# VectorE's order in the opening and the second group's period of a graph block, with two masks and two residual products moved from GpSimd

## The chip, the cores and the metric

The kernel runs on one core of one Trainium2 chip. The metric is the device time of one execution in microseconds (us). The kernel before takes 381.16 us, the median of three runs (380.99 to 382.29).

## The reference

32 graphs of 256 nodes with 128 features go through two blocks, each closed by a residual sum and a LayerNorm. `_layernorm` is without weights. Cut to what matters:

```
xc = transpose(x)                                              # block 1
h = relu(bn1(conv1(xc)));  h = bn2(conv2(h))                   # 1x1, then 17 taps over the nodes
x_conv = transpose(relu(h + xc))
s = x @ w_se.T + b_se                                          # 3 columns
A = exp(-(|s_n|^2 + |s_m|^2 - 2 s_n.s_m)) * adj
x_nmp = A @ relu(x @ w_msg.T + b_msg)
gi = [x_conv, x_nmp] @ w_ih.T + b_ih;  gh = x @ w_hh.T + b_hh
r, z = sigmoid(gi_r + gh_r), sigmoid(gi_z + gh_z);  n = tanh(gi_n + r * gh_n)
x = layernorm(x + (1 - z) * n + z * x)
h = relu(((1 + eps) * x + adj @ x) @ W1 + b1)                  # block 2
x = layernorm(x + h @ W2 + b2)
```

## The kernel before

The graphs go in 8 groups of 4, so 1024 columns, in two halves of 512 (`h` is 0 or 1). A period of the kernel (`steady(s)`) works on three groups at once: gates, normalisation and block 2 of group `s - 1` (`gb`), convolution and message part of group `s` (`gm`), and the first convolution of group `s + 1` (`gf`). `run` (L445) gives each engine `prologue()`, `steady(1)`, `steady(2)`, a hardware loop with two periods in it that runs twice, `steady(7)` and `last`. The order on each engine is written out by hand, and the engines meet at semaphores alone: `wait(engine, NAME, group, count)` and `done(instruction, NAME)`.

The 17 taps are computed from seven smaller sums (HALF, ZERO, PLUS2, MINUS2, PLUS1, MINUS1, INF), each with its stream of input differences (`sv`) and its 4 or 5 weights. Most products are made of three: an input is split into a high part (`sth`, `wh`, ScalarE's `stream_high`, `tap_high`) and the rest (`stl`, `wl`, VectorE's `stream_low`, `tap_low`), which costs one subtraction on VectorE with both inputs in SBUF. In the opening (group 0, and three sums of groups 1 and 2) TensorE uses the whole numbers (`plain_taps`, L1380); the low parts of the taps' weights are made in the first and second period, and TensorE waits for them by `w_low`, whose counts follow `W_ORDER` (L208).

The names that the change and the prediction touch:

- Masks: `exps` (ScalarE, L697) writes the exponentials. For groups 1 to 7 they stay in PSUM (`front`) and VectorE's `mask` (L968) multiplies them with `adjT` into `amat`. For group 0 they go to `amat` in SBUF and GpSimd's `first_mask` (L568) multiplies there. TensorE's `nmp` (L1441, `front<-amat,msg`) needs them.
- Residual product: `residual` (GpSimd, L552), `xw<-xw,xv`; VectorE's `gates_end` (L1043, L1046) needs it, and TensorE's `y_transpose` (L1495) needs that.
- Other work of GpSimd: `streams1`, `streams2` (L532, L533), `rsqrt` (L547, a power), `x_low1` (L573), `add_b2` (L562), `token_diffs` (L523, L525), `add_diagonal` (L581).
- VectorE: `reset` (L1032), `add_input` (L1038), `y_stats` (L1053, L1057), `y_apply` (L1075), `inf_stream` (L924, L928), `pair2_sum` (L991), `u_sum` (L981), `pair2_add` (L999, L1000), `pair1_sum` (L1004), `pair1_add` (L1012), `inf_add` (L1017), `xconv_low` (L1022), `nmp_low` and `stream_low` (L862), weights' low parts (L1115), sums for the opening's weights (L1159).
- TensorE: three-part products (L1327) of the gates (`back`, 27 of 512 columns for each half) and of the sums (`conv`, 12 or 15 of 256 columns), `aggregate` (L1441, `back<-adjT,xn`).

Order of TensorE in a period: HALF, ZERO, PLUS2, messages, gates of half 0, factors, gates of half 1, transpose of half 0, MINUS2, PLUS1, transpose of half 1, MINUS1, two distances, aggregate of both halves, two distances, INF, the MLP (with `conv1` of the next group between), `nmp` of both halves. The first three of these belong to the opening for group 1.

## Time and profile before

| | us |
| --- | --- |
| median of three runs | 381.16 |
| the profiled execution | 381.71 |
| its span, first to last instruction | 379.8 |
| TensorE busy | 363.1 (96%) |
| VectorE busy | 319.2 (84%) |
| ScalarE busy | 231.5 (61%) |
| GpSimd busy | 162.1 (43%) |
| share of TensorE in the chain that ended last | 66% |
| share of VectorE in it | 23% |

The granted clock of TensorE is 0.998 of full speed. The times of single instructions are from the profiled execution, from the start of its span. The end of a matmul is modelled, so matmuls overlap in the rows, and the distance from start to start tells what one costs. The opening lasts until the gates of group 0 start, at 43.7 us; the second group's period lasts from there to some 84.7 us, with its three opening sums of the next group to 91.6 us. The periods after it take 44 us each.

### The profile page before, as it was taken

To read this page: it belongs to the slowest core of one execution; us is meant where nothing else is said; L and a number is where in the kernel's file an instruction comes from. 1 tells how busy PE (TensorE), PEld (TensorE's weight loads), DVE (VectorE), ACT (ScalarE), POOL (GpSimd) and SP (SyncE) were. 2 spreads that over 40 slices of the span, in tenths; PEclk is the share of its full clock that TensorE was granted. 3 is DMA by queue.
4 is the path that set the end of the run, shared out by engine and by line. 5 is a ranking of instruction groups with operands and counts; after the bars stand their busy time and mean duration, and the time that the engine had idled before them with its cause. 6 is when DMAs were issued, how large, how long until landed. Compare 5 with 4: busy or idle time off the path is not lost.

```text
span 379.8 us, 6436 instructions
## 1 busy us (share of the span) xinstructions
PE 363.1 (96%) x2150; PEld 316.3 (83%) x2150; DVE 319.2 (84%) x702; ACT 231.5 (61%) x436; POOL 162.1 (43%) x162
## 2 busy tenths in 40 slices
PE   6999998899999999999999999999999999999994
PEld 4777887688898988899898998989888998988973
DVE  4999999998799987979699786998789886995584
ACT  3464773645767467664866567774676648564765
POOL 3125334446342653527323463517525373234362
PEclk9999999999999999999999999999999999999999
DMA  5700004300113010130112000120101201000002
GB/s 195 269 3 0 0 3 166 112 1 24 33 55 112 0 58 1 55 112 3 55 57 90 22 28 28 55 110 0 55 0 55 110 3 55 2 0 2 0 30 83
DMA packets 8135, 19.39 MB, mean 51 GB/s; under 512 B 688, under 2 KB 5168, under 8 KB 7088
## 3 DMA queue, kind: packets, MB, share of 16 engines
q1 hardware_dynamic: 7536, 18.17, 13.8%
q10 hardware_dynamic: 576, 0.92, 0.7%
q8 instruction: 13, 0.21, 0.2%
q14 instruction: 10, 0.08, 0.1%
HBM read 14.90 MB, written 4.19 MB: 50 GB/s over the span
## 4 chain that ended last, share of the span: by engine, by line
PE 66%; DVE 23%; issue 5%; DMA 3%; ACT 2%; POOL 1%; SPq 0%; ACTq 0%; DVEq 0%
PE back L1327 26%; PE conv L1327 17%; PE back L1441 6%; PE conv L1380 3%; DVE stats L1053 3%; PE back L1539 3%; DMA xv<-in_x_dram 3%; DVE stl L862 3%; PE front L1413 2%; DVE tail L1088 2%; PE back L1495 2%; PE front L1433 1%; DVE nmpl L862 1%; DVE sv L890 1%; DVE xn L1075 1%
## 5 line engine op out<-in xcount | busy, mean ns | idle before, releaser
L1327 PE MATMUL conv<-sth,wh 128*128 128x256 f32 x207 | 62.5, 302 | 1.3 <-DVE stl L862 1.2
L1327 PE MATMUL conv<-sth,wl 128*128 128x256 f32 x207 | 59.0, 285 | 0.0
L1327 PE MATMUL conv<-stl,wh 128*128 128x256 f32 x207 | 58.9, 284 | 0.0
L547 POOL TENSOR_TENSOR rstd<-rstd,small 128x4 f32<-128x4 f32 (+1 forms) x34 | 38.3, 1126 | 41.6 <-DVE rstd L1057 41.0
L1327 PEld LDWEIGHTS conv<-sth,wh 128*128 128x128 f32 x207 | 39.1, 189 | 3.5 <-DVE stl L862 1.2
L552 POOL TENSOR_TENSOR xw<-xw,xv 128x512 f32<-128x512 f32 (+1 forms) x17 | 21.2, 1246 | 47.9 <-ACT xw L720 47.9
L1327 PEld LDWEIGHTS conv<-stl,wh 128*128 128x128 f32 x207 | 39.1, 189 | 0.2
L1327 PEld LDWEIGHTS conv<-sth,wl 128*128 128x128 f32 x207 | 39.1, 189 | 0.0
L652 ACT ACTIVATE sth<-sv 128x272 fp32r<-128x272 f32 (+1 forms) x33 | 17.3, 523 | 35.6 <-DVE sv L890 20.9
L737 ACT ACTIVATE tail<-tail,shift,rstd 128x128 f32<-128x128 f32 x60 | 24.1, 482 | 11.2 <-DVE shift L1110 11.2
L581 POOL TENSOR_TENSOR adjT<-adjT,diag 128x256 f32<-128x256 f32 x32 | 27.9, 901 | 6.5 <-DVE msg L936 4.3
L1441 PE MATMUL back<-adjT,xn 128*128 128x256 f32 x120 | 28.2, 387 | 2.3 <-DVE xn L1075 2.1
L523 POOL TENSOR_TENSOR av<-h 128x544 f32<-128x544 f32 x6 | 8.1, 1342 | 51.4 <-ACT h L667 51.4
L1441 PE MATMUL front<-amat,msg 128*128 128x256 f32 x128 | 29.1, 379 | 0.0
L1441 PEld LDWEIGHTS back<-adjT,xn 128*128 128x128 f32 x120 | 22.0, 190 | 6.7 <-DVE xn L1075 2.9
L1539 PEld LDWEIGHTS back<-later_w,tail 128*128 128x128 f32 x224 | 26.3, 192 | 0.7
L1539 PE MATMUL back<-later_w,tail 128*128 128x128 f32 x224 | 26.5, 275 | 0.0
L744 ACT ACTIVATE tail<-back,first_w 128x512 f32<-128x512 f32 (+1 forms) x30 | 20.4, 683 | 9.7 <-PE back L1327 9.7
L1441 PEld LDWEIGHTS front<-amat,msg 128*128 128x128 f32 x128 | 23.8, 190 | 2.9
L1075 DVE TENSOR_SCALAR xn<-back,stats,rstd 128x128 f32<-128x128 f32 x60 | 20.5, 403 | 3.1 <-POOL rstd L547 2.4
L716 ACT ACTIVATE gbuf<-back,small 128x512 f32<-128x512 f32 x15 | 10.3, 690 | 19.3 <-PE back L1327 19.3
L562 POOL TENSOR_TENSOR tail<-xn,later_w 128x512 f32<-128x512 f32 x15 | 20.0, 1339 | 2.3 <-DVE xn L1075 2.3
(242 smaller groups left out, 1031.4 us busy)
## 6 DMA issues: line engine op xcount, KB each, us to landing
adjT<-in_adj_dram SPq DMA_DIRECT2D x8, 1024.0 KB, 4.9
out_dram<-tail SPq DMA_DIRECT2D x15, 256.0 KB, 2.2
xv<-in_x_dram SPq DMA_DIRECT2D x7, 512.0 KB, 3.3
tail<-in_conv_dram ACTq DMA_DIRECT2D x3, 256.0 KB, 4.6
gbuf<-in_gates_dram SPq DMA_DIRECT2D x1, 576.0 KB, 8.0
xv<-in_x_dram SPq DMA_DIRECT2D x2, 256.0 KB, 5.6
tail<-in_conv_dram SPq DMA_DIRECT2D x1, 320.0 KB, 5.4
later_w<-in_later_dram SPq DMA_DIRECT2D x1, 320.0 KB, 5.1
```

Source lines behind the costliest of these rows:

```text
L547: done(pool.tensor_tensor(rstd[:, k, v, q], rstd[:, k, v, q], minus_half[:, q], ALU.pow), RSTD[k])
L552: done(pool.tensor_tensor(xw[:, h, part(c)], xw[:, h, part(c)], xv[u][:, part_cols(h, c)], ALU.mult), XWX_READY)
L562: done(pool.tensor_tensor(out_tile(h, c)[:, q, :], xn[:, h, q, :], b2bc.unsqueeze(1).to_broadcast([P, len(part_blocks(c)), D]), ALU.add), ...
L581: done(pool.tensor_tensor(dg, dg, diag[:, :].unsqueeze(1).to_broadcast([P, PAR, P]), ALU.add), ADJE_READY)
L652: done(act.activation(dst, src, ACT.Copy), name)
L737: last = act.activation(o[:, q, :], o[:, q, :], ACT.Identity, bias=shift[:, v, q:q + 1], scale=rstd[:, 1, v, q:q + 1])
L744: done(act.activation(hid[:, h, f, part(c)], bank("hid", h, c, f), ACT.Relu, bias=vec[:, B1 + f:B1 + f + 1]), HID_READY)
L862: done(dve.tensor_tensor(dst, src, full(hi), ALU.subtract), name)
L1075: last = dve.tensor_scalar(xn[:, h, q, :], src(q, q + 1), stats[:, 0, v, q, 1:2], rstd[:, 0, v, q:q + 1], ALU.subtract, ALU.mult)
L1327: ins = pe.matmul(bank, a, b, start=first and k == 0, stop=last and k == len(todo) - 1)
L1441: ins = pe.matmul(tile[:, k * N:(k + 1) * N], lhs(b, rm), rhs(b, rm), start=rm == 0, stop=rm == PAR - 1)
L1539: ins = pe.matmul(tile[:, k * P:(k + 1) * P], hid[:, h, f, q * P:(q + 1) * P], w2[:, f, :], start=f == 0, stop=f == 1)
```

## The change

On VectorE:

- The masks of graphs 2 and 3 of group 0 go from GpSimd to VectorE, which reads the exponentials from PSUM. A semaphore of its own, `first_masked`, counts GpSimd's two masks, and `nmp` of group 0 waits for both kinds.
- Both residual products of group 0 go from GpSimd to VectorE.
- In the opening `pair1_sum` comes before `pair2_add`, and the low part of PLUS1's weights goes behind `factors` of the second period. ScalarE's wait for it goes from ahead of the gates to just ahead of the write of `tz` that needs it.
- The second group's period has its own function, `second_group`, with another order. The low part of ZERO's weights goes from ahead of half 1's `reset` to behind `pair2_sum`, and `inf_stream` from behind `gates_end` of half 1 to behind the first two masks. GpSimd waits for ZERO's low part ahead of `add_b2`, and ScalarE's high part of the INF stream goes behind the first two exponentials.
- At each period's end but the seventh, `inf_add` goes from between the two `nmp_low` to directly behind `pair1_add`, `xconv_low` of parity 0 from ahead of `half_stream` to behind both `nmp_low`, and the low parts of the pair-2 streams (`stream_low(gf, 2)`) ahead of `nmp_low`.

On VectorE in the opening, from `u_sum` of group 0 (L981 before, L995 after) to the differences of group 1; before:

```order
L981 SCALAR_TENSOR_TENSOR usum<-conv,first_w,xv 128x4x64 x4
L985 SCALAR_TENSOR_TENSOR usum<-conv,first_w,usum 128x4x64
L991 SCALAR_TENSOR_TENSOR pm<-conv,first_w,pm 128x4x64 x2
L884 TENSOR_TENSOR sv<-vv 128x272
L1159 SCALAR_TENSOR_TENSOR adjT<-adjT 128x640
L877 TENSOR_TENSOR av<-h 128x4x2x68
```

And after:

```order
L995 SCALAR_TENSOR_TENSOR usum<-conv,first_w,xv 128x4x64 x4
L999 SCALAR_TENSOR_TENSOR usum<-conv,first_w,usum 128x4x64
L982 TENSOR_TENSOR amat<-front,adjT 128x512
L1005 SCALAR_TENSOR_TENSOR pm<-conv,first_w,pm 128x4x64 x2
L898 TENSOR_TENSOR sv<-vv 128x272
L1177 SCALAR_TENSOR_TENSOR adjT<-adjT 128x640
L982 TENSOR_TENSOR amat<-front,adjT 128x512
L891 TENSOR_TENSOR av<-h 128x4x2x68
```

The two masks (`amat<-front,adjT`) stand where there was none; the last weight sum of the opening (`adjT<-adjT`) stands between them.

On VectorE in the second group's period, from the last sum of the gates of half 1 (L1046 before, L1064 after) to the low part of the INF stream (`stl<-sv,sth` of 272 columns); before:

```order
L1046 TENSOR_TENSOR gbuf<-gbuf,xw 128x512
L924 SCALAR_TENSOR_TENSOR sv<-av 128x4x67
L928 SCALAR_TENSOR_TENSOR sv<-sv 128x272
L1075 TENSOR_SCALAR xn<-back,stats,rstd 128x128 x4
L1053 BN_STATS stats<-back 128x6 x2
L1057 TENSOR_SCALAR rstd<-stats 128x4
L991 SCALAR_TENSOR_TENSOR pm<-conv,first_w,pm 128x4x64 x2
L1075 TENSOR_SCALAR xn<-back,stats,rstd 128x128 x4
L862 TENSOR_TENSOR stl<-sv,sth 128x272
L968 TENSOR_TENSOR amat<-front,adjT 128x512 x2
L1115 TENSOR_TENSOR wl<-tail,wh 128x512
```

And after:

```order
L1064 TENSOR_TENSOR gbuf<-gbuf,xw 128x512
L1093 TENSOR_SCALAR xn<-back,stats,rstd 128x128 x4
L1071 BN_STATS stats<-back 128x6 x2
L1075 TENSOR_SCALAR rstd<-stats 128x4
L1005 SCALAR_TENSOR_TENSOR pm<-conv,first_w,pm 128x4x64 x2
L1133 TENSOR_TENSOR wl<-tail,wh 128x512
L1093 TENSOR_SCALAR xn<-back,stats,rstd 128x128 x4
L982 TENSOR_TENSOR amat<-front,adjT 128x512 x2
L938 SCALAR_TENSOR_TENSOR sv<-av 128x4x67
L942 SCALAR_TENSOR_TENSOR sv<-sv 128x272
L1133 TENSOR_TENSOR wl<-tail,wh 128x512
L876 TENSOR_TENSOR stl<-sv,sth 128x272
```

The two instructions of the INF stream (`sv<-av`, `sv<-sv`) went behind the normalisation and the two masks; the first `wl<-tail,wh` is ZERO's.

On VectorE at the end of a period, from the second `out_stats` to the shifts; before:

```order
L1057 TENSOR_SCALAR rstd<-stats 128x4
L862 TENSOR_TENSOR nmpl<-front,nmph 128x512
L1017 SCALAR_TENSOR_TENSOR usum<-conv,first_w,usum 128x4x64
L862 TENSOR_TENSOR stl<-sv,sth 128x544
L862 TENSOR_TENSOR nmpl<-front,nmph 128x512
L1022 SCALAR_TENSOR_TENSOR xcl<-usum,xch 128x4x128
L1110 SCALAR_TENSOR_TENSOR shift<-stats,rstd 128x4 x2
```

And after:

```order
L1075 TENSOR_SCALAR rstd<-stats 128x4
L876 TENSOR_TENSOR stl<-sv,sth 128x544
L876 TENSOR_TENSOR nmpl<-front,nmph 128x512 x2
L1036 SCALAR_TENSOR_TENSOR xcl<-usum,xch 128x4x128 x2
L1128 SCALAR_TENSOR_TENSOR shift<-stats,rstd 128x4 x2
```

The low part of the pair-2 streams comes first, `inf_add` (`usum<-conv,first_w,usum`) stands no longer here, and both `xcl` stand together.

The diff, cut to its core:

```
-        W_ORDER = ("conv1", "gates", PLUS1, MINUS2, ZERO, MINUS1, INF, "w1", HALF, PLUS2)
+        W_ORDER = ("conv1", "gates", PLUS1, MINUS2, MINUS1, ZERO, INF, "w1", HALF, PLUS2)
-        A_READY = stage("a_ready", 4)
+        A_READY = stage("a_ready", 4, 0, 2)
+        def early(g, b):
+            return opening(g) and b < 2
...
# sync, prologue
-                wait(sp, A_READY, 0, 1)
+                sp.wait_ge(first_masked, 2)
+                wait(sp, A_READY, 0, 4)
...
# gpsimd
-                for b in range(GB):
-                    first_mask(b)
+                first_mask(0)
+                first_mask(1)
...
-                residual(gb, 1 - u, 0)
-                residual(gb, 1 - u, 1)
+                if not first:
+                    residual(gb, 1 - u, 0)
+                    residual(gb, 1 - u, 1)
                 rsqrt(0, gb, 0)
                 if first:
                     x_low1(0)
                 rsqrt(0, gb, 1)
                 if first:
                     x_low1(1)
+                    pool.wait_ge(w_low, w_count(ZERO))
                 add_b2(gb, 0)
...
# scalar
-                out = amat[...] if opening(g) else fb[b % 2][:, :]
+                out = amat[...] if early(g, b) else fb[b % 2][:, :]
...
                 wait(act, Z_FULL, g, item(h, c) + 1)
+                if opening(g) and h == 0:
+                    act.wait_ge(w_low, w_count(PLUS1))
...
                 minus2_out(gm)
-                stream_high(gm, 4)
+                if not first:
+                    stream_high(gm, 4)
                 if front:
                     x_high(gf, 1 - u)
                 minus1_out(gm)
                 exps(gm, 0)
                 exps(gm, 1)
+                if first:
+                    stream_high(gm, 4)
...
# vector
+            def residual(g, u, h):
+                wait(dve, XW_READY, g, h + 1)
+                done(dve.tensor_tensor(xw[:, h, :], xw[:, h, :], xv[u][:, cols(h)], ALU.mult), XWX_READY)
...
                 u_sum(0, 0)
+                mask(0, 0, 2)
                 pair2_sum(0)
                 first_stream1(MINUS1, ALU.subtract)
                 taps_step(minus1, minus1, -1.0, even)
+                mask(0, 0, 3)
...
+                pair1_sum(0)
                 pair2_add(0)
-                pair1_sum(0)
...
+                xconv_low(0, 1)
                 x_low(0, 0, 1)
-                tap_low(PLUS1)
-                xconv_low(0, 1)
+            def second_group():
+                messages(1, 0); messages(1, 1); messages(1, 2); factors(1)
+                tap_low(PLUS1); reset(0, 0); parts1(1)
+                add_input(0, 0); residual(0, 0, 0); gates_end(0, 0)
+                stream_low(1, 2); tap_low(MINUS2); stream_low(1, 3); tap_low(MINUS1)
+                reset(0, 1); add_input(0, 1); y_stats(0, 0); residual(0, 0, 1); gates_end(0, 1)
+                y_apply(0, 0); y_stats(0, 1); pair2_sum(1); tap_low(ZERO); y_apply(0, 1)
+                mask(1, 1, 0); mask(1, 1, 1); inf_stream(1); tap_low(INF); stream_low(1, 4)
+                h_low(0, 0); w_low_part(w1l...); h_low(0, 1)
+                mask(1, 1, 2); mask(1, 1, 3); u_sum(1, 1); pair1_sum(1)
...
                 pair1_add(gm, 1)
+                inf_add(gm)
...
                     out_stats(gb, 0)
-                    xconv_low(gm, 0)
                     half_stream(gf)
                     zero_stream(gf)
                     stream_low(gf, 0)
                     parts2(gf)
                     stream_low(gf, 1)
                     out_stats(gb, 1)
+                    stream_low(gf, 2)
                     nmp_low(gm, 0)
-                    inf_add(gm)
-                    stream_low(gf, 2)
                     nmp_low(gm, 1)
+                    xconv_low(gm, 0)
                     xconv_low(gm, 1)
...
# tensor
                 if opening(g):
-                    wait(pe, E_READY, g, h + 3)
-                    wait(pe, A_READY, g, 2 * h + 2)
-                else:
-                    wait(pe, A_READY, g, h + 3)
+                    pe.wait_ge(first_masked, 2)
+                wait(pe, A_READY, g, h + 3)
```

In the diff several calls of `second_group` stand on one line here; in the kernel each has its own.

## Rows read from the trace of the kernel before

**Rows 1.** windows of the steady periods, one period (stretch, its us, busy us of each engine, clock).

```profile
135.90:180.00 44.10, 43.91 (x274) 38.97 (x273) 36.99 (x83) 28.37 (x54) 19.73 (x19) 1.00 0.14 49
```

**Rows 2.** chain that ended last (start us, us, what).

```profile
151.08 3.65 PE conv L1327 x30
...
181.75 6.24 PE back L1327 x27
```

**Rows 3.** TensorE's waits (engine line <- waited for: us, times, longest).

```profile
PE back L1441 <- DVE xn L1075: 2.1, 2, 1.4
...
PE conv L1327 <- DVE stl L862: 1.2, 5, 0.4
```

**Rows 4.** timeline of TensorE (start us, us, what, idle before it and its releaser).

```profile
31.93 2.41 PE L1380 MATMUL conv<-sv,adjT 128*128 128x256 f32 x10 [0.95 <-DVE adjT L1159]
...
62.11 0.63 PE L1495 MATMUL back<-ident_w,gbuf 128*128 128x128 f32 x4 [1.16 <-DVE gbuf L1046]
...
71.61 0.39 PE L1327 MATMUL conv<-sth,wh 128*128 128x256 f32 x1
...
89.31 2.41 PE L1380 MATMUL conv<-sv,first_w 128*128 128x256 f32 x10 [0.74 <-issue]
```

**Rows 5.** timeline of VectorE in the opening.

```profile
28.71 1.27 DVE L884 TENSOR_TENSOR sv<-vv 128x272 f32<-128x272 f32 x1
29.90 1.88 DVE L1159 SCALAR_TENSOR_TENSOR adjT<-adjT 128x640 f32<-128x640 f32 x1
...
35.64 1.25 DVE L1000 SCALAR_TENSOR_TENSOR usum<-pm,usum 128x512 f32<-128x512 f32 x1
```

**Rows 6.** timeline of GpSimd in the opening.

```profile
25.93 5.18 POOL L568 TENSOR_TENSOR amat<-amat,adjT 128x512 f32<-128x512 f32 x4 [9.87 <-ACT amat L697]
```

**Rows 7.** timeline of VectorE in the second group's period.

```profile
50.17 1.26 DVE L1032 SCALAR_TENSOR_TENSOR gbuf<-gbuf 128x512 f32<-128x512 f32 x1
...
52.15 1.87 DVE L1115 TENSOR_TENSOR wl<-adjT,wh 128x640 fp32r<-128x640 f32 x1
...
57.17 1.92 DVE L1115 TENSOR_TENSOR wl<-adjT,wh 128x640 fp32r<-128x640 f32 x1
...
61.27 0.69 DVE L1046 TENSOR_TENSOR gbuf<-gbuf,xw 128x512 f32<-128x512 f32 x1
...
62.35 1.41 DVE L928 SCALAR_TENSOR_TENSOR sv<-sv 128x272 f32<-128x272 f32 x1
63.68 1.36 DVE L1075 TENSOR_SCALAR xn<-back,stats,rstd 128x128 f32<-128x128 f32 x4
64.95 0.75 DVE L1053 BATCH_NORM_STATS2 stats<-back 128x6 f32<-128x256 f32 x2
...
68.31 1.44 DVE L862 TENSOR_TENSOR stl<-sv,sth 128x272 fp32r<-128x272 f32 x1
69.67 1.28 DVE L968 TENSOR_TENSOR amat<-front,adjT 128x512 f32<-128x512 f32 x2
```

**Rows 8.** timeline of GpSimd there.

```profile
57.06 1.34 POOL L552 TENSOR_TENSOR xw<-xw,xv 128x512 f32<-128x512 f32 x1 [3.73 <-ACT xw L720]
...
62.03 1.43 POOL L573 TENSOR_TENSOR xl<-xv,xh 128x512 fp32r<-128x512 f32 x1
...
68.18 2.70 POOL L562 TENSOR_TENSOR tail<-xn,later_w 128x512 f32<-128x512 f32 x2
```

**Rows 9.** timeline of VectorE at a period's end.

```profile
176.69 0.48 DVE L1017 SCALAR_TENSOR_TENSOR usum<-conv,first_w,usum 128x256 f32<-128x256 f32 x1
177.08 0.72 DVE L862 TENSOR_TENSOR stl<-sv,sth 128x544 fp32r<-128x544 f32 x1
```

**Rows 10.** timeline of ScalarE there and in the gates after it.

```profile
175.98 0.66 ACT L652 ACTIVATE sth<-sv 128x544 fp32r<-128x544 f32 x1 [1.97 <-POOL sv L533]
...
184.57 0.69 ACT L713 ACTIVATE gbuf<-back,small 128x512 f32<-128x512 f32 x1
```

**Rows 11.** timeline of TensorE there.

```profile
177.85 0.39 PE L1327 MATMUL conv<-sth,wh 128*128 128x256 f32 x1 [0.19 <-DVE stl L862]
```

More of the change, by code:

```diff
@@ L804, in steady @@
                     msg_out(gm, k)
[L805 to L806 removed]
+                first = isinstance(s, int) and s == 1
                 gates(gb, 0)
@@ L1205, in prologue @@
                 w_low_part(wl[:, S_GATE:S_GATE + 9, :], graw, wh[:, S_GATE:S_GATE + 9, :], w_count("gates"))
+                xconv_low(0, 1)
                 x_low(0, 0, 1)
-                tap_low(PLUS1)
-                xconv_low(0, 1)
+            def second_group():
+                messages(1, 0)
+                messages(1, 1)
+                messages(1, 2)
+                factors(1)
+                tap_low(PLUS1)
+                reset(0, 0)
+                parts1(1)
+                add_input(0, 0)
+                residual(0, 0, 0)
+                gates_end(0, 0)
+                stream_low(1, 2)
+                tap_low(MINUS2)
+                stream_low(1, 3)
+                tap_low(MINUS1)
+                reset(0, 1)
+                add_input(0, 1)
+                y_stats(0, 0)
+                residual(0, 0, 1)
+                gates_end(0, 1)
+                y_apply(0, 0)
+                y_stats(0, 1)
+                pair2_sum(1)
+                tap_low(ZERO)
+                y_apply(0, 1)
+                mask(1, 1, 0)
+                mask(1, 1, 1)
+                inf_stream(1)
+                tap_low(INF)
+                stream_low(1, 4)
+                h_low(0, 0)
+                w_low_part(w1l[:, :], w1raw, w1h[:, :], w_count("w1"))
+                h_low(0, 1)
+                mask(1, 1, 2)
+                mask(1, 1, 3)
+                u_sum(1, 1)
+                pair1_sum(1)
@@ L1210, in steady @@
             def steady(s, u, front):
                 gb, gm, gf = s - 1, s, s + 1
-                first, second = isinstance(s, int) and s == 1, isinstance(s, int) and s == 2
-                for k in range(3):
-                    messages(gm, k)
-                factors(gm)
-                parts1(gm)
-                if first:
-                    stream_low(gm, 2)
-                reset(gb, 0)
-                add_input(gb, 0)
-                if first:
-                    tap_low(MINUS2)
@@ L1223, in steady @@
-                gates_end(gb, 0)
-                stream_low(gm, 3)
-                if first:
-                    tap_low(ZERO)
-                    reset(gb, 1)
-                    tap_low(MINUS1)
-                else:
+                if isinstance(s, int) and s == 1:
+                    second_group()
+                else:
+                    for k in range(3):
+                        messages(gm, k)
+                    factors(gm)
+                    parts1(gm)
+                    reset(gb, 0)
+                    add_input(gb, 0)
+                    gates_end(gb, 0)
+                    stream_low(gm, 3)
@@ L1232, in steady @@
                     reset(gb, 1)
[L1233 to L1257 removed]
+                    add_input(gb, 1)
+                    y_stats(gb, 0)
+                    gates_end(gb, 1)
+                    y_apply(gb, 0)
+                    y_stats(gb, 1)
+                    pair2_sum(gm)
+                    y_apply(gb, 1)
+                    stream_low(gm, 4)
+                    mask(gm, u, 0)
+                    mask(gm, u, 1)
+                    h_low(gb, 0)
+                    pair1_sum(gm)
+                    h_low(gb, 1)
+                    mask(gm, u, 2)
+                    mask(gm, u, 3)
                 if front:
@@ L1263, in steady @@
                 pair1_add(gm, 1)
-                if second:
+                inf_add(gm)
+                if isinstance(s, int) and s == 2:
                     tap_low(HALF)
```

43 lines of the change are left out of this document (10 added, 33 removed).

## The prediction

> **What bounds the kernel now.** I first read the windows. In a steady period of 44.1 us TensorE is busy for 43.9, at full granted clock, and VectorE for 37.0 [rows 1]. So from the third group on only what TensorE still waits for can be won. The chain of waits shows what TensorE costs there: 30 matmuls of 256 columns take 3.65 us, 0.122 each, and 27 of 512 columns take 6.24, 0.231 each [rows 2]. The list of TensorE's waits then names the two that matter beyond the opening: five times the low part of a stream, 1.2 us in all, and twice the normalised `xn`, 2.1 us [rows 3]. The timeline gives their places. TensorE stands before MINUS1 of the opening (0.95), before the second transpose of the second group's period (1.16), and before PLUS2 of group 2 (0.74) [rows 4]; the two waits for `xn` lie between the transpose at 62.11 and INF at 71.61. The bound is thus TensorE, with VectorE's order in front of it up to some 90 us.
>
> Why VectorE is late there stands in rows 5 to 8. `sv<-vv` on 272 columns takes 1.27 us and the weight sum after it 1.88 [rows 5], while GpSimd multiplies its four masks for 5.18 us [rows 6]; alone, such operations take 0.44 and 0.83 (the same forms elsewhere in the trace). The pattern repeats in the second group: 1.26, 1.87, 1.92, 1.41 and 1.44 us [rows 7], each over a two-input operation of GpSimd such as those at 57.06, 62.03 and 68.18 [rows 8]. VectorE's operation ends a short time after GpSimd's. The masks on VectorE at 69.67, with one input in PSUM, run beside GpSimd's `add_b2` at 0.64 each and lose nothing [rows 7, 8].
>
> The Trainium skill (SBUF — State Buffer, Who interferes with whom) says that a VectorE instruction with two SBUF inputs contends with a GpSimd instruction that reads SBUF, and that whoever issues first holds the shared pair of ports for the whole instruction. On VectorE's side this trace agrees: 1.92 us against some 0.83 for the one issued 0.11 us behind GpSimd's product [rows 7, 8]. The same rule speaks against a part of this change, since the two residual products have both inputs in SBUF on VectorE too; what that costs is in the sum below from rows.
>
> **The change, part by part.** Opening. VectorE gets two masks of 0.6 us each (half of 1.28, started back to back [rows 7]). GpSimd's masks end after two, at 25.93 + 2.6 = 28.5 [rows 6], so the stream and the weight sum lose their stalls, 0.83 and 1.05 [rows 5]. With one mask ahead of it the weight sum ends at about 30.6 instead of 31.8. TensorE is at MINUS1 at 30.8 by its own work and starts there instead of at 31.93 [rows 4]: 1.1 us. The next stream of differences comes only 1.9 - 1.2 = 0.7 us earlier, and TensorE waits for it at HALF of group 1, which gives back about 0.2. Opening: 0.9 us. The new wait of `nmp` for VectorE's mask 2 costs nothing: the mask ends at 28.6, `nmp` starts at 29.1; mask 3 ends at 31.2, its `nmp` comes near 35.5. Queued behind that wait is all of TensorE, so if mask 2 were late, each tenth would count.
>
> Second group up to the second transpose. VectorE: 0.7 earlier from the opening; 0.3 more since a PSUM operation (`pair1_sum`) now stands beside GpSimd's streams instead of L1000 at 1.25 against 0.68 [rows 5], halved because `pair2_add` still meets the second one; 0.6 for ZERO's low part that goes behind; 2.7 for the stalls of 0.58, 1.05 and 1.1 at L1032 and twice L1115 [rows 7], since GpSimd has no residuals and `reset` now runs before its streams. Against that: two residual products, 1.3; one of them beside the second of GpSimd's streams, 0.7 (as L1032 at 1.26 [rows 7]); 0.15 of waiting for the gates at `add_input`. That is -0.7 - 0.3 - 0.6 - 2.7 + 1.3 + 0.7 + 0.15 = -2.15. The last sum of the gates ended at 61.27 + 0.6 = 61.9 [rows 7]; now at 59.7. TensorE reaches the transpose at 62.11 - 1.3 - 0.9 = 59.9 (the stall from start to start is 1.3: 1.16 idle and what the modelled end hides). So this wait goes, just.
>
> From there to INF. TensorE needs 71.61 - 62.11 = 9.5 [rows 4] less the 2.1 for `xn` [rows 3]: INF could start at 59.9 + 7.4 = 67.3. VectorE's list in the new order: normalisation of half 0, 1.3 (63.68 to 64.95); statistics, `pair2_sum`, normalisation of half 1, 3.4 (64.95 to 68.31) [rows 7], with ZERO's low part in it for 0.3 more, since half of its 0.6 fills a wait for the power; two masks 1.2; the INF stream 0.9; INF's low weights 0.6 and low stream 0.4: 8.1 us. The INF stream has both inputs in SBUF and now stands where GpSimd runs `add_b2` twice for 2.70 [rows 8]; it waits for the end of one, 1.0, as `stl` did at 68.31 (1.44 against 0.44) [rows 7]. So 59.7 + 9.1 = 68.8 and TensorE starts INF at about 68.8 instead of 71.61: 2.8 to 2.9 us with the opening in it. `xn` is ready in time and no longer the last. What is late next is this low stream. ScalarE's high part of it now waits ahead of `h_high`; that costs nothing of its own, as `h_low` stands behind the low stream anyway. The transfer of group 1's adjacency starts earlier, since MINUS1's low part comes earlier; SP's load of x behind it needs the residual at about 58, and both land ahead of their use, so 0.
>
> After INF, VectorE (masks, `u_sum`, `xl`) and TensorE (INF, MLP) shift together. HALF of group 2 keeps the gain: its stream still waits for GpSimd's differences, which move with `conv1`. `inf_add` comes early, so PLUS2's wait goes: 0.74 idle and the hidden part, 0.9 [rows 4].
>
> Period ends. Before, ScalarE's high part is ready at 175.98 + 0.66 = 176.64 [rows 10], but VectorE does `nmp_low` and `inf_add` (176.69, 0.48) first, and `stl` runs from 177.08 to 177.80; TensorE starts at 177.85 after 0.19 idle [rows 9, 11]. A matmul lasts 0.28 in the rows and costs 0.12, so idle hides 0.16 more: 0.35 lost. Now `stl` starts at 176.65 at the latest, and up to 0.5 sooner, because 0.6 of `xcl` is gone from ahead of the half stream (GpSimd's differences limit that). It ends by 177.35, when TensorE wants it at 177.5. For five ends: 1.2 + 5 x 0.16 = 2.0 us [rows 3]. `inf_add` moves into a stretch in which VectorE waits for the MLP, 1.7 us idle: nothing; if that cover were gone, 0.4 for each period. The two `xcl` behind `nmp_low` delay the output shift by at most 0.6, on which the rival below rests.
>
> Sum: 2.85 + 0.9 + 2.0 = 5.75 us. The profiled execution took 381.71 (its span 379.8), so 375.95; the median of the runs is 0.55 below that execution, so **375.4 us**. Bounds of what no row shows: the stall of the INF stream lies between 0 (TensorE's own 67.3, 1.5 us more gain) and that of two GpSimd operations (1.4 more loss); the residual product between 0.6 alone and 1.3 with a stall. The own range of this case is 374.2 to 376.8.
>
> **Rivals.** *The port falls the other way.* GpSimd's power of half 0 starts at 57.6 and takes 1.0 to 1.4; then comes `x_low1`, 1.43 long [rows 8], while the last sum of the gates is due at 58.95. If GpSimd is first, the sum ends 1.1 later, the transpose waits 0.9, INF starts near 69.9, and `add_b2` may hold the INF stream again: gain 5.75 - 1.1 to 5.75 - 2.5, so 376.5 to 377.9. For it: two starts within 0.2 us, which I can't tell apart. Against it: the power is long beside VectorE's SBUF work. The skill's rule on issue order gives the same: whoever is first decides. Chance 0.2.
>
> *All of it is covered.* The INF stream slips between GpSimd's operations and TensorE is never late: 5.75 + 1.5 = 7.25, so 373.9. Chance 0.14.
>
> *The change does not do what it says at the period ends.* If another wait sets PLUS2 there (GpSimd's streams, of which ScalarE's row shows the wait of 1.97 [rows 10]), 2.0 us are missing and perhaps as much again at INF: 377.4 to 379.4. Against it: 0.4 us lay between high part and `stl`. Chance 0.07.
>
> *Slower.* The output shift comes late in each of six periods, ScalarE's normalisation and messages push the reset gate's tanh, which ends at 184.57 + 0.69 = 185.26 [rows 10], while TensorE needs it after 21 of the gates' matmuls, 181.5 + 4.9 = 186.4 [rows 2]. The slack is 1.15 us; I count 0.2 to 0.6 of delay. From 1.15 on each period pays. With 2.5 us of delay it is 1.35 x 6 = 8.1 against a gain of 5.75: 383.5. It decides the sign from a delay of 2.1 us. Nothing in the trace asks for so much. Chance 0.04. Another 0.05 is for a time within the measurement's noise by gains that cancel. The rest, 0.5, is the forecast.
>
> **How the numbers follow.** A measurement of this kernel tells 0.5% (1.9 us) from no change. The forecast, the first two rivals and all but the edge of the third are faster than 379.25: 0.5 + 0.2 + 0.14 + 0.07 = 0.91, of which I keep 0.9. Same 0.06, slower 0.04. The range reaches from just below the fully covered case to the port's rival with both losses: 373.4 to 378.4.
>
> **What would show it.** MINUS1 of the opening at 30.8 and the gates' start at 42.8 instead of 43.7; no idle before the second transpose near 59.9; the two masks of group 0 on VectorE at 0.6 each; INF near 68.8, led by `stl`; the INF stream at some 1.4 us; no TensorE wait for `stl` at the period ends, and periods of 43.7 instead of 44.05. The prediction is wrong if the residual products on VectorE stall for more than GpSimd's did, if INF starts at 71 or later, or if a period stays at 44 us.

## The result, and the profile after

The changed kernel takes 378.71 us (median of six runs, 377.08 to 380.05) and the kernel before 381.18 (six runs beside them, 380.99 to 382.29): a ratio of 0.993, interval 0.9913 to 0.9946. It is faster by 2.5 us, not by the 5.75 that were forecast, and the forecast's range ended at 378.4. The profiled execution took 380.05 (span 378.2), the longest of the six, so it shows the losses at their fullest.

TensorE's waits in it (engine line <- waited for: us in total, times, longest) answer to [rows 3]:

```profile
PE conv L1438 <- DMA xv<-in_x_dram: 2.0, 1, 2.0
PE conv L1368 <- DVE wl L1133: 1.7, 1, 1.7
PE back L1368 <- ACT gbuf L723: 1.3, 2, 1.1
PE front L1588 <- POOL tail L594: 1.3, 1, 1.3
PE back L1482 <- DVE xn L1093: 0.8, 1, 0.8
```

The five waits for `stl` are gone, one of the two for `xn` is gone, and so are those before MINUS1 and the second transpose. Two are new. One is for `wl`, VectorE's low parts ahead of INF, 1.7 us. The other is for `gbuf` from ScalarE's line 723: the tanh of the reset gate. It held TensorE twice.

TensorE's timeline (start us, us, what, idle before it and its releaser) at the places of [rows 4], with two of the gates' matmuls behind the new wait:

```profile
31.56 0.81 PE L1421 MATMUL conv<-sv,adjT 128*128 128x256 f32 x3
...
60.80 0.63 PE L1534 MATMUL back<-ident_w,gbuf 128*128 128x128 f32 x4
...
69.60 0.36 PE L1368 MATMUL conv<-sth,wh 128*128 128x256 f32 x1 [1.66 <-DVE wl L1133]
...
72.05 0.63 PE L1368 MATMUL back<-nmpl,w1h 128*128 128x512 f32 x1
72.48 0.63 PE L1368 MATMUL back<-nmph,w1l 128*128 128x512 f32 x1
...
74.28 0.39 PE L1368 MATMUL back<-nmpl,w1h 128*128 128x512 f32 x1
74.50 0.39 PE L1368 MATMUL back<-nmph,w1l 128*128 128x512 f32 x1
...
87.46 2.33 PE L1421 MATMUL conv<-sv,first_w 128*128 128x256 f32 x10
...
97.54 0.50 PE L1368 MATMUL back<-nmph,wh 128*128 128x512 f32 x1 [1.07 <-ACT gbuf L723]
...
141.93 0.51 PE L1368 MATMUL back<-nmph,wh 128*128 128x512 f32 x1 [0.25 <-ACT gbuf L723]
```

MINUS1, the second transpose and PLUS2 no longer wait. INF starts at 69.60 instead of 71.61. But look at the 512-column matmuls after it: from 72.05 to 72.48 is 0.43 us, where [rows 2] have 0.231, and at 74.28 the step is 0.22 again. The windows say why (stretch, its us, busy us and instructions of TensorE, its weight loads, VectorE, ScalarE and GpSimd, granted clock, DMA share, GB/s):

```profile
9.00:12.40 3.40, 3.40 (x11) 2.38 (x11) 2.75 (x5) 1.69 (x4) 0.00 (x0) 0.51 0.78 250
...
60.00:80.00 20.00, 18.34 (x110) 15.81 (x109) 19.66 (x41) 9.96 (x20) 6.67 (x6) 0.91 0.24 92
...
70.50:73.90 3.40, 3.40 (x13) 2.92 (x12) 3.40 (x9) 1.13 (x2) 0.00 (x0) 0.50 0.34 145
...
174.00:218.00 44.00, 44.00 (x275) 38.97 (x275) 38.44 (x84) 28.06 (x53) 19.78 (x19) 1.00 0.15 49
```

Twice the granted clock is 0.50, the level of 1.2 GHz: once in the opening, behind 2.0 us without work in which TensorE waits for the first loads, and once behind the wait before INF. The profile of before has 1.00 in both places, in the opening behind a wait of 1.8 us for the same loads.

The best way to see what each of these costs is to take one matmul of the program in both traces and to subtract its starts. The changed kernel is 0.84 us *late* from 13 us on (the low clock of the opening; in the profiles without it, the kernels of this study are 0 to 0.6 us early there, by when their first loads land), 0.37 early at MINUS1, 1.31 at the second transpose, 2.01 at the start of INF, 0.59 at 74 (1.42 lost to the low clock), 1.85 at PLUS2 of group 2, 0.69 behind the tanh at 97.54 (1.24 lost), 0.49 behind 141.93 (0.42 lost), then 0.74, 1.08, 1.34, 1.58 at the later period ends.

VectorE, to be read against [rows 5, 7]:

```profile
29.85 0.43 DVE L898 TENSOR_TENSOR sv<-vv 128x272 f32<-128x272 f32 x1
30.20 0.82 DVE L1177 SCALAR_TENSOR_TENSOR adjT<-adjT 128x640 f32<-128x640 f32 x1
...
50.79 0.89 DVE L1045 TENSOR_TENSOR xw<-xw,xv 128x512 f32<-128x512 f32 x1
51.66 1.20 DVE L1061 TENSOR_TENSOR gbuf<-gbuf 128x512 f32<-128x512 f32 x1
...
59.96 0.69 DVE L1064 TENSOR_TENSOR gbuf<-gbuf,xw 128x512 f32<-128x512 f32 x1
...
66.57 1.49 DVE L938 SCALAR_TENSOR_TENSOR sv<-av 128x268 f32<-128x268 f32 x1
...
68.46 0.68 DVE L1133 TENSOR_TENSOR wl<-tail,wh 128x512 fp32r<-128x512 f32 x1
69.06 0.43 DVE L876 TENSOR_TENSOR stl<-sv,sth 128x272 fp32r<-128x272 f32 x1
...
87.65 0.73 DVE L876 TENSOR_TENSOR stl<-sv,sth 128x544 fp32r<-128x544 f32 x1 [0.46 <-ACT sth L662]
88.30 1.28 DVE L876 TENSOR_TENSOR nmpl<-front,nmph 128x512 fp32r<-128x512 f32 x2
89.49 1.86 DVE L1036 SCALAR_TENSOR_TENSOR xcl<-usum,xch 128x512 fp32r<-128x512 f32 x2
91.28 0.76 DVE L1128 SCALAR_TENSOR_TENSOR shift<-stats,rstd 128x4 f32<-128x4 f32 x2
```

Stream and weight sum of the opening lost their stalls (0.43 and 0.82 against 1.27 and 1.88). The first operation of the INF stream took 1.49. At the period's end the output shift (line 1128) is last in a row of four. GpSimd at the three places where VectorE is held:

```profile
51.09 1.22 POOL L538 TENSOR_TENSOR sv<-vv 128x272 f32<-128x272 f32 x1
...
65.27 2.50 POOL L567 TENSOR_TENSOR tail<-xn,later_w 128x512 f32<-128x512 f32 x2
...
88.26 3.69 POOL L589 TENSOR_TENSOR adjT<-adjT,diag 128x256 f32<-128x256 f32 x4
```

And ScalarE, which waits for that shift (compare [rows 10]):

```profile
86.96 0.66 ACT L662 ACTIVATE sth<-sv 128x544 fp32r<-128x544 f32 x1 [1.95 <-POOL sv L538]
...
92.00 3.20 ACT L749 ACTIVATE tail<-tail,shift,rstd 128x128 f32<-128x128 f32 x8 [3.38 <-DVE shift L1128]
...
96.81 0.67 ACT L723 ACTIVATE gbuf<-back,small 128x512 f32<-128x512 f32 x1
```

ScalarE has nothing to do for 3.38 us, then normalises the output, builds the messages, and reaches the tanh at 96.81. It ends at 97.48; TensorE would have needed it at 97.54 - 1.24 = 96.30.

### The profile page after: what moved, and what is told of

Read it like the earlier page. It is cut to its first block, busy times and chain, and to the rows that moved or that the text cites. A ratio compares the mean times of both kernels' runs of the same rounds, so it can differ in the third digit from the quotient of the medians.

```text
span 378.2 us, 6430 instructions
## 1 busy us (share of the span) xinstructions
PE 364.7 (96%) x2150; PEld 317.2 (84%) x2150; DVE 322.8 (85%) x706; ACT 230.0 (61%) x436; POOL 154.1 (41%) x158
## 4 chain that ended last, share of the span: by engine, by line
PE 73%; DVE 13%; ACT 6%; POOL 3%; issue 2%; DMA 2%; SPq 0%; ACTq 0%; DVEq 0%
PE back L1368 24%; PE conv L1368 20%; PE back L1482 6%; PE front L1482 5%; PE back L1578 5%; PE conv L1421 3%; PE front L1454 2%; ACT tail L749 2%; PE front L1474 2%; DMA xv<-in_x_dram 2%; PE back L1534 2%; DVE xcl L1036 1%; DVE xn L1093 1%; ACT tail L756 1%; DVE stl L876 1%
## 5 line engine op out<-in xcount | busy, mean ns | idle before, releaser
L557 POOL TENSOR_TENSOR xw<-xw,xv 128x512 f32<-128x512 f32 (+1 forms) x15 | 18.5, 1234 | 46.9 <-ACT xw L732 46.9
L1050 DVE SCALAR_TENSOR_TENSOR gbuf<-gbuf 128x512 f32<-128x512 f32 (+1 forms) x17 | 13.6, 800 | 9.1 <-ACT gbuf L723 9.1
L876 DVE TENSOR_TENSOR stl<-sv,sth 128x272 fp32r<-128x272 f32 (+1 forms) x33 | 18.4, 557 | 3.0 <-ACT sth L662 2.9
```

Of the source, the lines that this page charges most:

```text
L557: done(pool.tensor_tensor(xw[:, h, part(c)], xw[:, h, part(c)], xv[u][:, part_cols(h, c)], ALU.mult), XWX_READY)
L876: done(dve.tensor_tensor(dst, src, full(hi), ALU.subtract), name)
L1050: done(dve.scalar_tensor_tensor(ghn[:, h, part(c)], tr[:, h, part(c)], 1.0, ghn[:, h, part(c)], ALU.add, ALU.mult), T1_READY)
```

## The experiments

Two theories stood against each other. *The tanh*: the late output shift costs what the forecast misses. *The clock*: the stall before INF costs more than its wait, because TensorE then runs at 1.2 GHz. Both rest on the trace of one execution, so each is taken away alone and with the other.

**The kernel before, again (r_before).** No edit; it gives the noise.

> The kernel before, unchanged, to see how often its runs have a stretch at the low TensorE clock. Theory (half of the missing gain is clock: the changed kernel's 1.7 us wait before INF is followed by a stretch at half clock, cost 1.4 us): the kernel before shows a granted clock of 0.998 or more in at least four of its six runs. Rival (these stretches come at random in both kernels): it shows 0.990 to 0.995 in half of its runs and the same scatter, some 3 us, as the changed kernel. Time 381.2 us.

381.27 us (380.93 to 382.12, 12 runs), ratio 0.9997, interval 0.9988 to 1.0007. All executions of this kernel in the study lie between 380.7 and 382.6 us, with mean granted clocks of 0.991 to 1.0. Its profile has no low stretch inside. Neither expectation came as it was written: 4 of the 12 runs have 0.998 or more, but only one is below 0.995. Over all the runs of this kernel whose clock is on record, 6 of 63 have a mean of 0.994 or less, and they took 382.05 to 382.55 us; in the changed kernel it is 4 of 6.

**Output shift first (e_shift).** The changed kernel with another order at the period's end:

```diff
                     stream_low(gf, 2)
+                    out_shift(gb, 0)
                     nmp_low(gm, 0)
                     nmp_low(gm, 1)
+                    out_shift(gb, 1)
                     xconv_low(gm, 0)
                     xconv_low(gm, 1)
-                    out_shift(gb, 0)
-                    out_shift(gb, 1)
```

> The changed kernel with the two output shifts of VectorE moved forward in each period's end: the first ahead of both nmp_low, the second ahead of both xcl. Theory (the late shift delays ScalarE's normalisation, the messages' relu and the reset gate's tanh, for which TensorE waits 1.24 us in period 2, 0.42 in period 3 and about 0.1 in each later one): these waits vanish, 1.24 + 0.42 + 4 x 0.1 = 2.0 us less than the changed kernel, so 376.7 us, periods from the third on of 43.7 us. Rival (ScalarE is late by its own work, not by the shift): under 0.5 us, and the wait for the tanh in period 2 stays near 1 us.

376.38 us (374.79 to 377.14, 6 runs), ratio 0.9857, interval 0.9834 to 0.9879. The wait for `gbuf` is gone. ScalarE starts the normalisation 4 us earlier and the tanh 3.3 us earlier (1.1 of each is not from the edit: this execution has no low clock in the opening, and TensorE is at PLUS2 at 86.36 instead of 87.46):

```profile
87.95 3.19 ACT L749 ACTIVATE tail<-tail,shift,rstd 128x128 f32<-128x128 f32 x8 [0.42 <-DVE shift L1128]
...
93.53 0.69 ACT L723 ACTIVATE gbuf<-back,small 128x512 f32<-128x512 f32 x1
```

The same matmuls of two successive periods are 43.57 us apart, against 43.77 in the changed kernel and 44.05 before. So the late shift still cost some 0.2 in each of the later periods, where the list of waits shows nothing. The stall before INF (1.6) and the low clock behind it are in this profile too. Its two runs at a mean clock of 0.997 and 0.998 took 374.85 and 374.79; the four at 0.989 to 0.994 took 376.26 to 377.14.

**Work in the stall (e_fill).** The changed kernel with seven matmuls of 256 columns, without use, ahead of the wait before INF of the second group's period:

```diff
                 if first:
+                    for _ in range(7):
+                        pe.matmul(bb[0][:, 0:2 * P], ident,
+                                  traw[PLUS2][:, 0:2, :].rearrange("p k o -> p (k o)"), start=True, stop=True)
                     pe.wait_ge(w_low, w_count(INF))
```

> The changed kernel with seven extra matmuls of 256 columns on TensorE, into a bank that the MLP overwrites, between the last distances and INF of the second group's period, where TensorE waits 1.7 us. They change no result. Theory (the idle time there brings the stretch at half clock at 70.5 us): no slow stretch near 70 us in the profile, clock 0.995 or more in nearly all runs, INF starts at the same time, and the median is 0.7 to 1.4 us lower, 377.5. Rival (the slow stretch comes from elsewhere): same clock as before the edit and the median unchanged, 378.7.

378.94 us (378.48 to 379.11, 6 runs), ratio 0.9932, interval 0.9918 to 0.9946. TensorE's timeline and the window:

```profile
67.06 3.29 PE L1650 MATMUL back<-first_w,ident_w 128*128 128x256 f32 x14
70.00 0.47 PE L1368 MATMUL conv<-sth,wh 128*128 128x256 f32 x1
```

```profile
60.00:80.00 20.00, 20.00 (x123) 17.44 (x123) 19.62 (x42) 10.61 (x20) 6.65 (x6) 1.00 0.21 76
```

The clock is 1.00, in all six runs the mean is 0.996 to 0.999, and their spread shrank from 3.0 us to 0.6. The seven matmuls ran as 14 and took 3.0 us, about 1.3 more than the stall they fill. So the median is no better, and not at the 377.5 that I had expected: what the clock gave back went to the filler. As a fix it is worthless; as evidence it separates the two costs, for the wait for the tanh (1.4) is still there.

**Both (e_shift_fill).** The edits of e_shift and e_fill together.

> Both edits together, shifts forward and the filler matmuls. If the two losses are separate, the gains add: 2.0 + 1.2 = 3.2 us under the changed kernel, 375.5 us. If the filler's busy time only moves the slow clock to another place, it equals the shift edit alone, 376.7.

376.4 us (376.22 to 377.28, 5 runs), ratio 0.9879, interval 0.9861 to 0.9897. Against e_fill, with the same filler, the shift edit is worth 378.94 - 376.4 = 2.5 us. That is the tanh's price with the clock mostly out of play. Mostly: two of the five runs took 377.2 and 377.3 us at mean clocks of 0.994 and 0.993, although the stall is filled. Where their low stretch lay, no trace shows; the profiled run (0.995) has none while TensorE works.

**Period ends alone (e_ends_only).** The kernel before with only the new order at the end of each period:

```diff
                 pair1_add(gm, 1)
+                inf_add(gm)
...
                     out_stats(gb, 0)
-                    xconv_low(gm, 0)
                     half_stream(gf)
...
+                    stream_low(gf, 2)
                     nmp_low(gm, 0)
-                    inf_add(gm)
-                    stream_low(gf, 2)
                     nmp_low(gm, 1)
+                    xconv_low(gm, 0)
                     xconv_low(gm, 1)
...
                 else:
-                    inf_add(gm)
```

> The kernel before with the new order at the period ends alone. Theory (the ends save the five waits for the low stream, 2.0 us, and the wait before PLUS2, 0.9, and bring a late output shift for which TensorE waits at the gates): 381.3 - 2.9 + about 0.5 of new waits for the tanh = 378.9 us, with a wait for ScalarE's gbuf in period 2 that is shorter than the 1.1 of the changed kernel, since TensorE is less far ahead there. Rival (the late shift belongs to the new order of the second group, not to the ends): no wait for the tanh, 378.4 us.

380.04 us (379.65 to 380.2, 6 runs), ratio 0.9962, interval 0.9949 to 0.9975. The `stl` waits and the one of PLUS2 are gone, and the tanh's is there in full, with no other part of the change:

```profile
PE back L1440 <- DVE xn L1075: 2.1, 2, 1.4
...
PE back L1326 <- ACT gbuf L713: 1.3, 2, 1.1
```

I had expected it to be shorter, since TensorE is less far ahead here; that fell. The gain is 1.1 to 1.2: the 2.9 forecast for the period ends and PLUS2, less 1.25 + 0.42.

**All but the period ends (e_front_only).** The changed kernel with the old order there, the reverse of the diff above.

> The changed kernel with the old order at the period ends, so the opening and the second group's part alone. Theory: the two parts add, apart from the wait for the tanh, which needs both (TensorE ahead and the shift late): opening 0.9 and INF 2.0 to 2.8 us, less a stretch at half clock of 1.4 in a good half of the runs; 381.3 - 2.9 + 0.8 = 379.2 us, no wait for the tanh over 0.3. Rival (the wait for the tanh comes from TensorE being ahead alone): it stays at 1 us in period 2.

379.85 us (378.29 to 381.1, 12 runs), ratio 0.9959, interval 0.9944 to 0.9974. The waits in which VectorE's old end has its part are back, the tanh's is absent, and the stall before INF is there:

```profile
PE conv L1369 <- DVE wl L1133: 1.7, 1, 1.7
...
PE conv L1369 <- DVE stl L876: 1.2, 5, 0.4
```

Its runs at a mean clock of 0.998 took 378.29 to 378.75, those at 0.989 to 0.994 took 379.6 to 381.1. The better ones gain 2.4 to 2.9, where 2.85 was forecast for this part; the others lose about 1.6 of it (medians 378.35 and 379.96).

**add_b2 later (e_addb2).** If the stall of VectorE's INF stream is the cause of TensorE's stall, taking GpSimd from beside it must shorten both. The shift edit, and GpSimd waits for a later low part of the weights before its two `add_b2`:

```diff
-                    pool.wait_ge(w_low, w_count(ZERO))
+                    pool.wait_ge(w_low, w_count("w1"))
```

> The shift edit and one more: GpSimd starts its two add_b2 of the second group's period only when W1's low part is there, instead of ZERO's. Theory (the INF stream's first operation waits 1.05 us on VectorE for GpSimd's add_b2): it takes 0.44 instead of 1.49, INF starts 1.0 us earlier, TensorE's wait before it falls from 1.6 to 0.6 us, and the stretch at half clock goes from most runs: 374.8 (the runs of the shift edit without that stretch) - 1.0 = 373.8 us. Rival (the operation is slow by its own shape): still 1.4, and 376.4 us.

**373.85 us** (373.72 to 374.38, 5 runs), ratio 0.9806, interval 0.9792 to 0.9821: the best kernel of the study, 7.4 us below the kernel before and 4.9 below the changed one. The theory had expected 373.8. VectorE, GpSimd, TensorE and the window:

```profile
65.25 0.43 DVE L938 SCALAR_TENSOR_TENSOR sv<-av 128x268 f32<-128x268 f32 x1
```

```profile
68.24 2.58 POOL L567 TENSOR_TENSOR tail<-xn,later_w 128x512 f32<-128x512 f32 x2 [4.25 <-DVE w1l L1133]
```

```profile
67.21 0.36 PE L1368 MATMUL conv<-sth,wh 128*128 128x256 f32 x1 [0.59 <-DVE wl L1133]
```

```profile
60.00:80.00 20.00, 19.41 (x118) 16.82 (x118) 19.59 (x42) 10.79 (x21) 8.97 (x8) 1.00 0.20 66
```

The stream takes 0.43 instead of 1.49, TensorE's idle time falls from 1.6 to 0.59, exactly by that, the profile has no low stretch behind it, and no run has a mean clock below 0.995.

**ZERO's low weights later too (e_zero_late).** e_addb2, and the low part of ZERO's weights (VectorE, with its high part on ScalarE, where INF and ZERO change places, as they do in `W_ORDER`) behind the low part of the INF stream, to take the last 0.59. On VectorE:

```diff
                 pair2_sum(1)
-                tap_low(ZERO)
...
                 stream_low(1, 4)
+                tap_low(ZERO)
                 h_low(0, 0)
```

> As the add_b2 edit, and ZERO's low weights (0.6 us on VectorE) come behind the low part of the INF stream, with the places of ZERO and INF changed in the order of weights. Theory (VectorE's list from the gates to INF is what TensorE waits for): INF starts another 0.6 us earlier and TensorE's wait there is nearly gone; behind it conv1 waits for xl by up to 0.5, so 0.2 to 0.6 us below the add_b2 edit, 373.4 us, no stretch at half clock. Rival: the wait just moves to conv1, same time as the add_b2 edit.

374.58 us (374.08 to 374.97, 5 runs), ratio 0.9818, interval 0.9803 to 0.9833: not better. The wait for `wl` stays at 0.6, and a new one appears:

```profile
PE conv L1368 <- DVE wl L1133: 0.6, 1, 0.6
PE conv L1368 <- DVE xl L876: 0.3, 1, 0.3
```

On VectorE the place that ZERO's part left is in part idle, since the normalisation of half 1 now waits for GpSimd's power:

```profile
63.08 1.37 DVE L1093 TENSOR_SCALAR xn<-back,stats,rstd 128x128 f32<-128x128 f32 x4 [0.34 <-POOL rstd L552]
```

Counted from 12 us on, where the loads no longer matter, TensorE reaches INF 0.2 us earlier than in e_addb2 and PLUS2 0.3 later: what is put behind one wait of TensorE is missing at the next. The medians are 0.7 apart, but the intervals overlap, and in the two profiles half a microsecond of that is there before the first difference of the kernels.

**Masks alone (e_masks_only).** The kernel before with only the masks of graphs 2 and 3 on VectorE in the opening (`mask(0, 0, 2)` ahead of `pair2_sum(0)`, `mask(0, 0, 3)` behind the step of MINUS1, and GpSimd's loop of four cut to two).

> The kernel before with only the two masks moved: graphs 2 and 3 of group 0 on VectorE out of PSUM, GpSimd with two. Theory (VectorE gains 1.88 us of stalls for 1.2 us of masks): MINUS1 of the opening starts 1.1 us earlier, VectorE is 0.7 us ahead from there to the second group's low streams, and the whole is 0.6 to 0.9 us faster, 380.5 us. Rival (VectorE's gain is eaten by the next waits): MINUS1 earlier, but INF of the second group at its old place, 381.2 us.

380.46 us (379.97 to 381.55, 12 runs), ratio 0.998, interval 0.9969 to 0.9991. MINUS1 starts without a wait at 30.69, 1.24 earlier, of which 0.14 comes from the loads:

```profile
30.69 2.33 PE L1390 MATMUL conv<-sv,adjT 128*128 128x256 f32 x10
```

The kernel gains 0.8 (0.3 to 1.2 by the interval). The opening's term of 0.9 is right, and so is its working: 1.1 forecast at MINUS1 (30.8), and some of it given back behind it: from 12 us on the two profiles end 1.0 apart.

**Three filler matmuls (e_fill3).** e_shift with three instead of seven, to fill the stall without lengthening it.

> The shift edit and three extra matmuls (1.3 us of TensorE's work, less than its 1.9 us wait) between the last distances and INF of the second group's period. Theory (the seven extra matmuls took 3.0 us, longer than the wait, and so hid that the stretch at half clock was gone): INF starts when VectorE's low weights are there, at its place of the shift edit, no stretch at half clock in any run, 374.9 us in all runs, against the shift edit's 376.4 with both kinds. Rival (the wait and the clock are not tied): 376.4 and the same scatter of 2 us.

375.38 us (374.7 to 375.87, 5 runs), ratio 0.9842, interval 0.9824 to 0.986. INF starts at 68.64, 0.18 later than in e_shift, but so does all of the program from 12 us on: the filler delays nothing. The profile has no low stretch, and no run is below 0.995. The interval overlaps that of e_shift, and the 374.9 expected for all runs was not met; the ratio alone would not tell them apart. What tells is that the runs of 376.3 to 377.1 us at low mean clock are missing, and that from INF to 74 us this profile is 1.5 us ahead of e_shift's.

**Residual products back on GpSimd (e_res_pool).** e_addb2 with the two products of group 0 taken from VectorE.

```diff
-                if not first:
-                    residual(gb, 1 - u, 0)
-                    residual(gb, 1 - u, 1)
+                residual(gb, 1 - u, 0)
+                residual(gb, 1 - u, 1)
```

> The add_b2 edit (373.85 us) with both residual products of group 0 back on GpSimd, at their old place behind its streams. Theory (on GpSimd each holds the port for 1.3 us ahead of VectorE's work with two SBUF inputs, and the first comes late for the gates' last sum): VectorE is 1.2 us later at the second transpose and at INF, 375.0 us. Rival (VectorE saves two operations of 0.6 us, and GpSimd's products fall beside PSUM reads): the same or faster, 373.3 us.

374.38 us (373.95 to 375.74, 5 runs), ratio 0.9822, interval 0.9801 to 0.9843; e_addb2's is 0.9792 to 0.9821. The two intervals overlap, so whether this part of the change brings anything is not shown. It is 0.5 us at the medians, and 0.3 between the profiles from 12 us on. The profile of this kernel has the low stretch of the opening (8.8 to 12 us, behind 1.9 us of waiting for loads) and none at INF, whose stall is 0.7; a second run took 375.74 at a mean clock of 0.990. GpSimd's products, and VectorE waiting for the first:

```profile
51.38 1.76 POOL L557 TENSOR_TENSOR xw<-xw,xv 128x512 f32<-128x512 f32 x1
56.53 1.83 POOL L557 TENSOR_TENSOR xw<-xw,xv 128x512 f32<-128x512 f32 x1 [3.40 <-ACT xw L731]
```

```profile
53.17 0.69 DVE L1063 TENSOR_TENSOR gbuf<-gbuf,xw 128x512 f32<-128x512 f32 x1 [1.21 <-POOL xw L557]
```

VectorE's second sum of the gates comes at 59.59, 0.95 after that of e_addb2 (58.64), but the whole program is 1.0 later since the opening: it is not late, and the 1.2 us that the theory asked for are not there. On VectorE, the products take 0.89 and 0.68, and the operation behind the first is held besides (1.20 at 51.66 in the changed kernel). So the place of the products is nearly free either way, and the gain there must be from the order of `reset` and the streams; that order was not run alone.

## Why the prediction was wrong

**What held.** The opening: MINUS1 without a wait, 0.8 of 0.9 us (e_masks_only). The second transpose: the last sum ended at 60.65 in the profiled execution, which was 0.84 late by then, so 59.8 where 59.7 was forecast, and the wait is gone; the rival in which the power holds the sum did not come (0.69 at 59.96). INF: 69.60 - 0.84 = 68.76, forecast 68.8, led by `stl` and the low weights. The INF stream held by `add_b2`: 1.49, forecast 1.4. The Trainium skill (SBUF — State Buffer, Who interferes with whom: who issues first keeps the shared pair, the other blocks) is borne out at this place: GpSimd's second `add_b2` began at 66.50, VectorE's operation at 66.57, and in e_addb2 its 1.49 become 0.43 when GpSimd isn't there. PLUS2 of group 2 without a wait: the lead grows by 1.0, forecast 0.9. The five `stl` waits: gone; in e_shift, where the tanh doesn't hide it, TensorE's lead grows by 2.1 over the five period ends, forecast 2.0. Each of these terms is right within 0.1 or 0.2 us.

**The step that failed first** is the one sentence "The two `xcl` behind `nmp_low` delay the output shift by at most 0.6", against a slack of 1.15 (the slack is right: before, the tanh ended at 97.15 and TensorE needed it at 98.23). It counted the instructions moved ahead of the shift, 0.6, and nothing of when their row starts and what they meet:
- `stl` now stands right behind the statistics and waits 0.46 for ScalarE's high part (87.65). Before, `xcl`, `nmp_low` and `inf_add` filled that time. The early `stl` that I had booked as a gain brought idle time of VectorE ahead of the shift with it.
- The two `xcl` now stand beside GpSimd's `add_diagonal` (88.26 to 91.95): 1.86 instead of 1.2, 0.66 more. It is the second that is held (0.72 and 1.21); before, the only `xcl` there took 0.68.
- `inf_add` is gone from the row, -0.4, so the shift is 0.6 + 0.46 + 0.66 - 0.4 = 1.3 later against the half stream. This one started 1.0 earlier than before, and the shift still came 0.3 later.
- TensorE did not stand still meanwhile: at PLUS2 it gained the 1.0 of the term above. I held a late shift against TensorE's old place.

So the delay seen from TensorE is about 1.3 + 1.0 = 2.3 us against 1.15 of slack; it waits for 1.24 (e_ends_only has the same). The cost is 1.24 + 0.42 + some 0.2 in each later period: 2.1 us between the profiles of e_shift and the changed kernel from 12 us on, 2.3 by the two best runs of e_shift against the best one of the changed kernel (377.08 - 374.8), 2.5 by e_shift_fill against e_fill. The mechanism is that of the slower rival, chain and all, with a chance of 0.04. Its condition (a delay over 2.1) was met. Its price was not: it asked 1.35 in each of six periods, 8.1 in all, and the wait was 1.24, 0.42 and then a fraction, because TensorE, once held back, is no longer ahead. Why it is still 0.42 in the third period and not nothing I did not isolate.

**The second step that failed** is the price of the stall before INF. The forecast has TensorE able to start at 67.3 and starting at 68.8, and counts this as 1.5 us less gain. In the profile it is 1.66 idle and then a stretch at 1.2 GHz, and the matmuls from 69.60 to 74 lose 1.42. The prediction noted full clock in the steady periods and had no term for a fall of it. Before, the longest idle times of TensorE there were 1.4 and 1.16, and the profile shows 1.00 behind them. It isn't in every execution: of the changed kernel's six runs, two have a mean clock of 0.995 and 0.999 and took 377.37 and 377.08; the others 0.990 to 0.994 and 378.69 to 380.05. The Trainium skill (TensorE: Matmul & The Clock Gate, Part 1: The HAM clock gate) says that the moment of such a transition varies from run to run of one kernel, and that the clock has two levels; the runs agree with both (0.50 and 1.00 in the windows, and mean clocks of 0.990 to 0.999 for one kernel), and the rest of this paragraph stands on them alone. That it is the stall which brings the low clock at INF is shown by the profiles: all three with the stall of 1.6 to 1.7 have it (the changed kernel, e_shift, e_front_only), and none of those with the stall filled (e_fill, e_fill3, e_shift_fill) or short (e_addb2, e_zero_late, e_res_pool). By runs, 17 of 24 with the stall have a mean clock of 0.994 or less, and 4 of 31 without it, two in e_shift_fill and two in e_res_pool. One of these four is the profiled one of e_res_pool, whose low stretch is in the opening. The opening's low stretch, 0.84 us in the profiled execution, is behind a wait for loads that the change does not touch (2.0 us here, 1.9 in e_res_pool, the only other profile with it); the kernel before, with 1.8 in both of its profiles, did not show it, and I can't say whether the change makes it more frequent.

**The sum again.** 5.75 forecast, less 2.1 to 2.5 for the late shift, is 3.3 to 3.7. The changed kernel's best run is 377.08, 4.1 below the median of the kernel before and 3.9 below its best run beside it (380.99). The parts run alone add up the same way: 2.9 (e_front_only, best run) + 1.2 (e_ends_only) = 4.1. Less about 1.4 for the low clock in most runs, the median gain is 2.5. The 0.2 to 0.8 that are left over I can't place; the landing of the first loads alone moves the profiles by 0.6. The test of the forecast's own terms is e_fill3, the changed kernel without the late shift and without the low clock: 375.38 us, where 375.4 was forecast, and from 12 us on its profile gains 6.0 against the kernel before, where the terms add up to 5.75. So the sum was right as far as it went, and the two losses were missing from it.

With both failed steps mended, by two moved calls and one changed count, the gain is 7.4 us, more than forecast, since e_addb2 also takes the stall of the INF stream that the forecast had accepted.

## What to carry to other kernels

When a change takes waits away from the bounding engine, check every chain that feeds this engine one period later against its *new* place, not against its old one: idle time ahead, contention and the bounding engine's own gain add up, and here they made 2.3 us out of 0.6. A stall of TensorE can be paid twice, as idle time and as low clock behind it; and the number to watch is the spread of the runs with their clock. How long a stall must be for this is not shown here: 1.6 to 1.7 us at INF did it in most runs, and 1.8 in the opening of the kernel before did not in two profiles. Give an instruction that starts a long chain on another engine (here eight normalisations, messages and a tanh behind a shift of 4 elements for each partition) the first place in its engine's row.

## What the runs showed that I had not expected

- TensorE's granted clock fell to 0.50 (1.2 GHz) behind 1.6 to 1.7 us without work at INF, in all three profiles with that stall, while 1.16 and 1.4 us in the kernel before left it at 1.00, and so did 1.8 us in its opening. Work without use in the gap at INF kept it up.
- A plain fp32 matmul of 256 columns is two passes of 0.21 us in the records (14 for seven, 3.0 us), against 0.122 for one of the kernel's fp32r products of the same width [rows 2]. Three of them are six passes, so some 1.3 us, and a filler must be chosen by its measured time.
- GpSimd's residual product took 1.34 us beside VectorE before [rows 8], and 1.76 and 1.83 in e_res_pool, where a two-input operation of VectorE had begun just before each (at 51.23 and 56.52): whoever comes second is lengthened, and here that was GpSimd, by some 0.45, while VectorE's two took 0.73 and 0.68.
